# The tail of a convolution-attention-MoE kernel: layer products in halves, attention in quarters, gates by half of the tokens

## The reference, cut to what matters

```
# L0: softmax attention with 8 heads over the 1024 pixels of each image, output projection,
#     group norm, + x                                          (the first 195 us of the span)
t  = to_tokens(x)                                   # 2 images x 1024 tokens x 64 channels
Z  = ln(t)
for l in range(4):                                  # linear attention, 8 heads, 4 layers
    Z = Z + sum_j( (Z Q[l,j] Z^T) (Z V[l,j]^T) ) / 1024 / 8
t  = t + Z
u  = ln(t)
p  = softmax(u @ router_w + router_b)               # 8 experts, the two largest, renormalised
t  = t + sum over the top 2 of  p_e * (u @ expert_w[e] + expert_b[e])
```

## Time and profile before

| | |
|---|---|
| median of 3 | 244.69 us |
| profiled execution | 245.45 us |
| its span | 243.6 us |
| PE, DVE, ACT, POOL busy | 233.3, 199.7, 174.7, 45.8 us |
| layers begin (L792) | 201.67 us |
| attention over z (L821) | 215.04 us |
| first gate spread (L874) | 228.37 us |
| last expert product ends | 240.49 us |

### The profile page before, as it was taken

The page is one execution under the profiler, slowest core; times in us unless marked ns, Lnnn a source line. Parts: engine busy times, 40 slices in busy tenths (PEclk is TensorE's granted clock), DMA queues, the critical chain, the costliest instruction groups (busy, mean ns, idle before and its releaser), DMA issues.

```text
span 243.6 us, 6266 instructions
## 1 busy us (share of the span) xinstructions
PE 233.3 (96%) x2390; PEld 127.5 (52%) x2390; DVE 199.7 (82%) x424; ACT 174.7 (72%) x359; POOL 45.8 (19%) x83
## 2 busy tenths in 40 slices
PE   7999999999999999999999999999999998789994
PEld 6356455555455554545555555455444685558421
DVE  2699798999999999999999999999622683349873
ACT  2553738998999989989899988998996232229710
POOL 6965069400000002000000320000100000000250
PEclk9999999999999999999999999999999999999999
DMA  4005400051221221333300000000000000000002
GB/s 140 0 8 214 112 23 3 22 188 65 63 79 49 55 55 37 90 85 143 97 8 0 4 3 3 4 0 4 1 3 3 1 0 3 0 3 0 4 0 86
DMA packets 6082, 10.09 MB, mean 41 GB/s; under 512 B 2236, under 2 KB 3820, under 8 KB 5924
## 3 DMA queue, kind: packets, MB, share of 16 engines
q1 hardware_dynamic: 6052, 9.69, 13.0%
HBM read 6.84 MB, written 2.62 MB: 39 GB/s over the span
## 4 chain that ended last, share of the span: by engine, by line
PE 90%; DVE 4%; ACT 1%; issue 1%; DMA 1%; DVEq 0%; SPq 0%; ACTq 0%
PE psum L575 28%; PE psum L512 18%; PE psum L476 18%; PE psum L893 3%; PE psum L613 3%; PE psum L545 2%; PE psum L440 1%; PE psum L802 1%; DMA wqk_sb<-in_wqk 1%; PE psum L532 1%; PE psum L538 1%; PE psum L452 1%; PE psum L792 1%; PE psum L781 1%; PE psum L829 1%
## 5 line engine op out<-in xcount | busy, mean ns | idle before, releaser
L1256 DVE TENSOR_REDUCE half_max<-psum 128x1 f32<-128x512 f32 x256 | 157.0, 680 | 4.5 <-PE psum L476 3.8
L1087 ACT ACTIVATE probs<-psum 128x512 f32<-128x512 f32 x228 | 120.2, 605 | 13.9 <-PE psum L512 11.3
L476 PE MATMUL psum<-kop,qop 64*128 64x512 f32 x256 | 87.3, 440 | 0.3 <-DVE kop L1228 0.2
L512 PE MATMUL psum<-qop,kop 64*128 64x512 f32 x256 | 83.9, 441 | 0.5 <-ACT qop L1092 0.4
L575 PE MATMUL psum<-probs,v_aug 128*32 128x256 f32 (+1 forms) x1296 | 73.1, 341 | 0.2 <-DVE o_sb L1270 0.2
L512 PEld LDWEIGHTS psum<-qop,kop 64*128 64x128 f32 x256 | 39.5, 184 | 21.7 <-ACT probs L1087 10.7
L575 PEld LDWEIGHTS psum<-probs,v_aug 128*32 128x32 f32 x1296 | 32.3, 109 | 32.5 <-issue 22.2
L476 PEld LDWEIGHTS psum<-kop,qop 64*128 64x128 f32 x256 | 40.5, 184 | 16.4 <-DVE half_max L1256 9.2
L996 POOL CAST max_part<-negmax 128x8 fp32r<-128x8 f32 x13 | 2.5, 192 | 96.9 <-issue 85.1
L1037 POOL TENSOR_TENSOR early<-probs,early 128x512 f32<-128x512 f32 x4 | 5.1, 1272 | 57.8 <-ACT probs L1182 57.6
L1083 ACT ACTIVATE probs<-psum 128x1024 f32<-128x1024 f32 x14 | 13.4, 1028 | 0.3
(11 more groups left out here) (188 smaller groups left out, 197.1 us busy)
## 6 DMA issues: line engine op xcount, KB each, us to landing
parts_scratch<-early SPq DMA_DIRECT2D x4, 512.0 KB, 3.2
qop<-parts_scratch SPq DMA_DIRECT2D x28, 64.0 KB
vt_sb<-in_vt SPq DMA_DIRECT2D x1, 1024.0 KB, 4.9
kop<-parts_scratch SPq DMA_DIRECT2D x14, 64.0 KB
kop<-parts_scratch SPq DMA_DIRECT2D x28, 32.0 KB
x_sb<-in_x SPq DMA_DIRECT2D x2, 256.0 KB, 3.1
q_pair<-in_q_pairs SPq DMA_DIRECT2D x1, 512.0 KB, 3.4
qop<-max_row SPq DMA_DIRECT2D x26, 4.0 KB
```

Source lines behind the costliest of these rows:

```text
L476: last = nc.tensor.matmul(psum[:, m % MAX_BANKS, :], qop[at, b * PP + pp, qh * NH + t * P:qh * NH + (t + 1) * P], kop[at, b * PP + pp, c * ...
L512: last = nc.tensor.matmul(psum[:, bank, :], kop[at, b * PP + pp, mt * P:(mt + 1) * P], qop[at, b * PP + pp, qh * NH:(qh + 1) * NH], start= ...
L1087: last = nc.scalar.activation(probs[:, n % P_RING, h, :], psum[:, bank, :], ACT.Exp, scale=SCALE)
L1256: V.tensor_reduce(half_max[:, i, c, h * HT + t:h * HT + t + 1], psum[:, m % MAX_BANKS, :], AX_X, ALU.max, negate=True).then_inc(S["slot_fr ...
```

## The change

The layer product is issued in two halves of 128 columns: heads of the first half of both images into banks 7 and 5, those of the second into banks 0 and 2; ACT and DVE copy a half as it is done. The ACT copy of z's channels moves from behind `tt` of layers 0 and 1 to ahead of `tt` of layers 1 and 2. Attention over z goes in four quarters of 256 tokens over banks 0, 1, 6 and 7, and DVE adds in four pieces. For the gates, the largest logit is subtracted from all first, the second gate is `ed * gate1`, the product of the first gate with its one-hot is made on POOL (`first_gate`), and behind the second largest logit the two halves of the tokens no longer alternate: DVE finishes half 0 up to `gate_split`, then begins half 1. PE turns half 0 alone; half 1 is turned between experts(2) and experts(4). DVE makes the gates of half 1 (`split_gates(1)`, six instructions, each waiting for the one in front) behind its second expert job. The order of the experts' work on PE is written out.

```diff
+GV_BANKS = ((7, 5), (0, 2))
+T2_BANKS = (0, 1, 6, 7)
-GT_BANKS = (2, 5)
-GB_BANKS = (3, 4, 0, 1, 5, 2)
+GT_BANKS = (2, 7)
+GB_BANKS = (3, 4, 2, 5, 0, 1)
...
@@ PE, a layer
-                for b in range(B):
-                    for odd in range(2):
-                        last = nc.tensor.matmul(psum[odd * C:(odd + 1) * C, (7, 5)[b], 0:NHEAD // 2 * C],
-                                                gram[image(b), :], vt_sb[image(b), l, odd, :],
-                                                start=True, stop=True, skip_group_check=True)
-                    last.then_inc(S["gv_full"], 1)
+                for half in range(2):
+                    for b in range(B):
+                        for odd in range(2):
+                            last = nc.tensor.matmul(psum[odd * C:(odd + 1) * C, GV_BANKS[half][b], 0:2 * C],
+                                                    gram[image(b), :], vt_sb[image(b), l, odd, 2 * half * C:2 * (half + 1) * C],
+                                                    start=True, stop=True, skip_group_check=True)
+                        last.then_inc(S["gv_full"], 1)
...
@@ PE, attention over z
-            for c in range(2):
-                for b in range(B):
-                    last = nc.tensor.matmul(psum[image(b), c, :], tt_f[image(b), :], z_t[image(b), c * NH:(c + 1) * NH],
...
+                for b in range(B):
+                    last = nc.tensor.matmul(psum[image(b), T2_BANKS[i], 0:QB], tt_f[image(b), :],
+                                            z_t[image(b), i * QB:(i + 1) * QB], start=True, stop=True, skip_group_check=True)
...
@@ PE, experts
             broadcasts(0, 4)
+            pe.wait_ge(S["yt_ready"], YT_BANKS.index(MOE_BANKS[0]) + 1)
             expert_bias(0)
-            broadcasts(4, SCALED)
-            for first in range(0, len(MOE), B):
-                if first == len(MOE) // 2:
-                    expert_bias(1)
-                experts(first)
-                broadcasts(first + SCALED, min(first + SCALED + B, len(MOE)))
+            broadcasts(4, 6)
+            experts(0)
+            broadcasts(6, 8)
+            experts(2)
+            gates_to_channels(1)
+            experts(4)
+            broadcasts(8, 12)
+            experts(6)
+            expert_bias(1)
+            broadcasts(12, 14)
+            experts(8)
+            broadcasts(14, 16)
+            experts(10)
+            experts(12)
+            experts(14)
...
@@ POOL
+            pool.wait_ge(S["share_ready"], 2)
+            for c in range(2):
+                at = slice(c * TT, (c + 1) * TT)
+                nc.gpsimd.tensor_tensor(first_gate[:, at, :], hot1[:, at, :],
+                                        gate1[:, at].rearrange("p (a o) -> p a o", o=1).broadcast_to([P, TT, E]),
+                                        ALU.mult).then_inc(S["first_gated"], 1)
...
@@ DVE, gates
+            def split_gates(c):
+
+                link(V.tensor_tensor(of(hot2, c), of(hot2, c), over_e(dlt, c), ALU.mult))
+                dve.wait_ge(S["first_gated"], c + 1)
+                link(V.tensor_tensor(of(gates, c), of(first_gate, c), of(hot2, c), ALU.add))
+                link(V.tensor_copy(gp(0, c), by_tile(gates, c)))
+                link(V.tensor_tensor(by_tile(gate_rest, c), by_tile(gates, c), gp(0, c), ALU.subtract))
+                link(V.tensor_copy(gp(1, c), by_tile(gate_rest, c)))
+                V.tensor_tensor(gp(2, c), by_tile(gate_rest, c), gp(1, c), ALU.subtract).then_inc(S["gate_split"], 1)
...
@@ DVE, experts
                 V.tensor_tensor(scaled[:, i % SCALED, :], psum[:, GB_BANKS[i % len(GB_BANKS)], :],
                                 yt2[:, b, c * NH:(c + 1) * NH], ALU.mult).then_inc(S["scaled_dve"], 1)
+                if i == BY_DVE[1]:
+                    split_gates(1)
```

More of the change, by code:

```diff
@@ L845, in _, with gates_to_channels @@
             pe.wait_ge(S["logits_read"], 1)
-            for c in range(2):
+            def gates_to_channels(c):
                 pe.wait_ge(S["gate_split"], c + 1)
+                if c:
+                    pe.wait_ge(S["yt_ready"], YT_BANKS.index(GT_BANKS[1]) + 1)
                 for t in range(TT // 2):
@@ L1140, in _ @@
             for l in range(LAYERS):
[L1141 to L1144, removed]
+                for half in range(2):
+                    act.wait_ge(S["gv_full"], 4 * l + 2 * half + 1)
+                    nc.scalar.activation(gv[:, 0, 2 * half:2 * half + 2, :],
+                                         psum[:, GV_BANKS[half][0], 0:2 * C].rearrange("p (j c) -> p j c", c=C),
                                          ACT.Copy).then_inc(S["gv_act"], 1)
+                if l in (1, 2):
+                    act.wait_ge(S["zt_full"], l)
+                    nc.scalar.activation(z_t[:, (l - 1) * NH:l * NH], psum[:, PROJ_BANKS[l - 1], :], ACT.Copy).then_inc(S["zt_ready"], 1)
                 act.wait_ge(S["tt_full"], l + 1)
@@ L1380, in _ @@
             for l in range(LAYERS):
[L1381 to L1384, removed]
+                for half in range(2):
+                    dve.wait_ge(S["gv_full"], 4 * l + 2 * half + 2)
+                    V.tensor_copy(gv[:, 1, 2 * half:2 * half + 2, :],
+                                  psum[:, GV_BANKS[half][1], 0:2 * C].rearrange("p (j c) -> p j c", c=C)).then_inc(S["gv_dve"], 1)
                 dve.wait_ge(S["m_full"], l + 1)
@@ L1391, in _ @@
                     V.tensor_copy(gram[:], psum[:, 5, 0:C]).then_inc(S["gram_ready"], 1)
[L1392 to L1395, removed]
+            for i in range(4):
+                at = slice(i * QB, (i + 1) * QB)
+                dve.wait_ge(S["attn2_full"], i + 1)
+                V.tensor_tensor(t2[:, at], psum[:, T2_BANKS[i], 0:QB], t1[:, at], ALU.add).then_inc(S["t2_ready"], 1)
             token_rstd(2).then_inc(S["rstd_ready"], 1)
@@ L1440, in _ @@
+            halves(lambda c: V.tensor_tensor(of(hot1, c), over_tokens(weight_sb), over_e(pick, c), ALU.is_equal))
             halves(lambda c: V.scalar_tensor_tensor(out=of(lg2, c), in0=of(hot1, c), scalar=-3e38, in1=of(lg, c),
                                                     op0=ALU.mult, op1=ALU.add))
[L1442 to L1453, removed]
@@ L1454, in _ @@
-            halves(lambda c: V.tensor_tensor(of(gates, c), of(gates, c), over_e(gate1, c), ALU.mult))
-            dve.wait_ge(S["gate_zeroed"], 1)
+            for c in range(2):
+                dve.wait_ge(S["dve_chain"], chain[0] - 1 + c)
+                V.tensor_reduce(of(m2, c), of(lg2, c), AX_X, ALU.max).then_inc(S["delta_ready"], 1)
             def by_tile(v, c):
@@ L1462, in gp, with second_places @@
                 return gate_part[:, c * TT // 2:(c + 1) * TT // 2, :].rearrange("p t (b r) -> p t b r", b=B)[:, :, :, s * E:(s + 1) * E]
-            halves(lambda c: V.tensor_copy(gp(0, c), by_tile(gates, c)))
-            halves(lambda c: V.tensor_tensor(by_tile(gate_rest, c), by_tile(gates, c), gp(0, c), ALU.subtract))
-            halves(lambda c: V.tensor_copy(gp(1, c), by_tile(gate_rest, c)))
-            for c in range(2):
-                dve.wait_ge(S["dve_chain"], chain[0] - 1 + c)
-                V.tensor_tensor(gp(2, c), by_tile(gate_rest, c), gp(1, c), ALU.subtract).then_inc(S["gate_split"], 1)
+            def second_places(c):
+                dve.wait_ge(S["delta_ready"], c + 1)
+                link(V.tensor_tensor(of(cand, c), of(lg2, c), over_e(m2, c), ALU.is_equal))
+                link(V.tensor_tensor(of(cand, c), of(cand, c), over_tokens(weight_sb), ALU.mult))
```

55 lines of the change are left out of this document (33 added, 22 removed).

## The result

The changed kernel takes 250.94 us (median of 4, 248.12 to 251.52) against 244.88 for the kernel before: ratio 1.0196, 95% interval [1.0149, 1.0244]. It is slower, and by more than forecast: 246.9 was the forecast and 247.9 the end of its range.

The account below looks back on a forecast made before the run. PE was taken as busy nearly throughout, trading hand-overs with ACT and DVE in the layers and bounding alone from 226 us. Terms -0.8 - 0.1 + 2.8 + 0.2 + 0.1 = +2.2 on 244.69 gave 246.9 us; range 244.2 to 247.9.

Parts of the forecast that it names:

- rival 5: Experts: PE's new 2.7 us wait lets the clock fall, costing another 7 us, over 250; chance 0.03, outside the range.
- Layers: Four layers: with halves, copies and PE's sums start about 0.2 us sooner each, -0.8 us in all.
- Attention: Attention over z: quarters let DVE's first addition end sooner, but PE's own stream limits the gain to -0.1 us.
- Gates of half 0: Gates of the first half: PE does not wait for them, so making them sooner gains nothing; taken as 0.
- The hold: Gates of half 1: POOL's jobs 2 and 5 block DVE twice, delaying PE's experts(2) by 2.8 us; chance 0.42.
- Rivals 1 and 2: Gates of half 1: DVE not held by POOL, 244.7 us, chance 0.29; or held once, 245.7 us, chance 0.13.
- PE's own work and the end: Half 1's gate transposes and paired broadcasts on PE, +0.2 us; last DVE expert jobs beginning later, +0.1 us.

Follow-up runs that it names:

- e1: The changed kernel run again with no edit, and profiled a second time; 250.95 us (248.54 to 251.67, 6 runs).
- after: The first profile of the changed kernel, no further edit; the profiled execution took 251.52 us.
- e10: The changed kernel without its layer halves and attention quarters, keeping its gates and order of experts; 249.5 us, ratio 1.0181.
- e4: The changed kernel with 24 dummy matmuls on PE in its wait before the second expert pair; 249.63 us, ratio 1.0153.
- e9: The changed kernel with dummy matmuls both in the layers and in PE's wait before the second expert pair; 248.2 us, ratio 1.0132.
- e3: The kernel before with layer halves and attention in quarters, old gates and experts; 246.14 us, ratio 1.0017.
- e5: The changed kernel with POOL's expert jobs waiting until DVE has finished the gates of half 1; 247.3 us, ratio 1.0066.
- e2: The kernel before with the layer halves alone and the moved copy of z's channels; 246.06 us, ratio 1.0016.
- e7: The kernel before with layer halves and two or three dummy matmuls in each layer's PE waits; 244.69 us, ratio 0.9996.
- e8: The kernel before with layer halves, attention quarters and dummy matmuls in the layers, old gates and experts; 244.65 us, ratio 0.9977.
- e12: e8 run again: kernel before with layer halves, attention quarters and dummy matmuls in the layers; 244.61 us, ratio 0.9965.
- e6: The kernel before with tests added behind its end, kinds of DVE instruction alone and beside a POOL product; one execution, 257.96 us.
- e11: The changed kernel with e7's dummies, POOL's jobs 2 and 5 given to DVE, gates of half 1 behind job 3; 246.3 us, ratio 1.0035.

## Why the prediction was wrong

It was right in its sign and in the hold of DVE by POOL, and wrong in the rest of the size: it had priced a fall of the clock in one place at nothing, and had none in another.

*The step that failed: rival 5, "The clock falls in the new wait", with a chance of 0.03.* The prediction worked out PE's wait at 2.7 us, said that the trace had no such wait at the upper level, and then priced it at nothing. It does fall, in all three profiles with the wait and without dummies in it: 10.26 to 10.38 us for the last stage in e1, after and e10, against 8.79 with dummies (e4, e9), so **1.5 to 1.6 us**. The price the rival gave, 7 us, was wrong the other way: it doubled all seven pairs, while the clock came back behind two. With 1.6 on the forecast of 246.9 and no other stretch the result would have been 248.5. The changed kernel's one execution at 0.993, the clock of a profile with one such stretch, took 248.54, though which stretch it met no profile shows. The fall isn't certain either: one of its ten executions took 248.12 at a mean clock of 0.999, where e4's and e9's with dummies took 247.4 to 248.2, so it seems to have kept its clock. No profile caught it.

*What the prediction had nowhere: the clock in the attention product.* With the halves and without dummies in the layers, that product took 3.45 to 3.56 us in four of six profiles (e1, e3, e4, e5; not in after and e2) for 1.9, **1.6 us**. It needs the halves (no execution of e10's 5 or of the kernel before's 87 has the clock and time of one) and goes with dummies in the layers (no such execution in e7, e8 and e12). PE's busy share of the layers changed little, 10.82 of 13.37 us before, 10.29 of 12.88 after, so why the halves bring it on isn't shown; the count of executions is what stands behind it.

*Layers, -0.8 forecast, -0.49 measured.* The copies start when I said (0.55 behind the stage's start, DVE at 204.18). PE is later: from L801's second record (204.39) to its first sum it needs 0.2, where I put 0.1. The sums start 0.97 behind the stage's start instead of 1.02, and take 0.69 instead of 0.75: 0.12 a layer.

*Attention, -0.1*: measured -0.09 at equal clock (1.87 for 1.96).

*Gates of half 0, nothing*: right. Tokens to gates is 3.42 or 3.43 us in every kernel, and the gates stand behind the dummies as before.

*The hold, +2.8*: right in kind, twice and by whole POOL jobs, as read off the copies. Its own rows gave 234.3 - 231.56 = 2.74. Measured it is 2.48; another 0.13 lies in front of experts(0), where PE waits 0.59 for `gate_t` and 0.24 for job 0 (before 0.29 and 0.18), which no term had. Together PE lost 2.6. Rivals 1 and 2 are out by the two durations. The Trainium skill's rule (SBUF — State Buffer, section SBUF: two separate sides) for two SBUF inputs is borne out by e5 and e6. The same section of the Trainium skill has a figure of some 115 ns from DVE's end, for a DMA that had to wait for a DVE copy; it did not hold for POOL's job here, since job 5 started at 232.52, DVE's first gate instruction ended at 232.53 and its second started at 232.56. So the block came a second time, as the forecast had it.

*PE's own work and the end, +0.3*: 8.79 for 8.28 at equal clock, +0.5. The forecast had the wait for the last job at 0.1. In e9 DVE's last two expert jobs are done at 242.40:

```profile
241.13 1.27 DVE L1523 TENSOR_TENSOR early<-psum,early 128x512 f32<-128x512 f32 x2
```

and PE's last four records start at 242.55, 0.66 behind the ones in front where 0.43 is usual: 0.23.

The upper end of the range, 247.9, was called the forecast with the layers' gain gone; that is 246.9 + 0.8 = 247.7. The measured median lies beyond either.

At equal clock the measured terms are -0.5 - 0.1 + 2.6 + 0.5 = +2.5, for +2.2 forecast. The rest of the typical run, 1.6 in front of experts and 1.6 behind the wait, is clock.

## What to carry to other kernels

Before a DVE instruction that lives in SBUF is moved, look at what POOL runs there: a short one can take as long as POOL's whole instruction (1.30 us for 0.22 here), and a chain of short ones is held again by each of POOL's instructions that gets in between. A stage in which PE is the bound has nothing to give to work done sooner in front of it, and all to lose to work put between its feeders. And when a prediction finds a new long wait of PE (2.4 us here), a fall of the clock belongs in the sum; dummy matmuls in the waits show what it cost.

## What the runs showed of the hardware that I had not expected

- Kinds of DVE instructions held by POOL go beyond two inputs: a copy, a cast and a tensor_scalar of one SBUF input of 64 elements took 0.94 for 0.20, while tensor_reduce from SBUF wasn't held (0.21 for 0.22).
- A PE wait of 2.4 us was followed by half clock in after, e1 and e10 (though not, by its mean clock, in the execution of 248.12 us); one of 1.22 us (e5) and one of 0.89 (e11) were not.
- With the halves, which shorten a stage with many short waits from 13.37 to 12.88 us, 8 of 24 executions had the clock and time of a low stretch right behind it (none of 87 before); dummy matmuls in these waits took them away at no cost to the stage (12.88).
- Executions of the kernel before fall in groups: 67 of 87 at a clock of 1.00, others at 245.8 (clock 0.992), 247.6 (0.986) and 251.9 (0.965). Profiles of other versions suggest what they are: a low stretch at 192 us cost 0.8 (e9), one at 24 us 2.0 (the layers of the first profile began that much later), a longer one there 6.8 (e8). Five executions at 1.00 take 2 us more (247.3); no profile caught one, and what they are is open.
